# Causal attention and a product-key expert layer on one core: score products over 64 rows with one copy of the keys, and one mask product for each bank

## The reference

```
q, k, v = split((x @ w_qkv.T), 16 heads of 8)
q = rope(rms_norm(q, q_norm_w)); k = rope(rms_norm(k, k_norm_w))
attn = einsum('bhqd,bhkd->bhqk', q, k) * 8 ** -0.5
attn = where(causal, -inf, attn); attn = softmax(attn)
out = einsum('bhqk,bhkd->bhqd', attn, v) @ w_proj.T
x = layernorm(x + out)
# expert layer: xn = rmsnorm(x); q = xn @ w_q.T; s1, i1, s2, i2 = top 8 of 32 keys on two sides;
# fs = top 8 of the 64 sums; hidden = gelu(xn . expert_down[fi]) * relu(fs); y = sum hidden * expert_up[fi]
x = layernorm(x + y)
```

## Time and profile before

| | |
|---|---|
| median of 3 runs | 1785.13 us |
| the profiled execution, and its span | 1787.43 us, 1785.5 us |
| DVE busy | 1507.0 us, 84% |
| PE busy | 1353.2 us, 76% |
| ACT busy | 938.5 us, 53% |
| POOL busy | 750.4 us, 42% |
| mean granted PE clock | 0.818 of 2.4 GHz |

### The profile page before, as it was taken

The page is one execution under the profiler, slowest core; times in us unless marked ns, Lnnn a source line. Parts: engine busy times, 40 slices in busy tenths (PEclk is TensorE's granted clock), DMA queues, the critical chain, the costliest instruction groups (busy, mean ns, idle before and its releaser), DMA issues. The chain is left out here.

```text
span 1785.5 us, 53337 instructions
## 1 busy us (share of the span) xinstructions
PE 1353.2 (76%) x19632; PEld 929.3 (52%) x19632; DVE 1507.0 (84%) x6821; ACT 938.5 (53%) x1646; POOL 750.4 (42%) x1088
## 2 busy tenths in 40 slices
PE   3557588787968778796877869697887869688556
PEld 2323265554646555464645646474655546465436
DVE  2136898989899898989989899998989998988994
ACT  0647463755556475564647465564737555563110
POOL 1216353444635353453525355463534446352320
PEclk7688879797888879788887969888796978878665
DMA  3000000000000000000000000000000000000000
GB/s 77 1 6 8 6 8 8 14 8 1 15 7 15 7 14 8 1 15 7 15 7 14 8 2 15 6 15 7 15 8 14 8 1 15 1 15 1 8 7 9
DMA packets 29976, 18.59 MB, mean 10 GB/s; under 512 B 1824, under 2 KB 29216, under 8 KB 29728
## 3 DMA queue, kind: packets, MB, share of 16 engines
q1 hardware_dynamic: 29728, 15.23, 3.0%
HBM read 11.04 MB, written 4.19 MB: 9 GB/s over the span
## 5 line engine op out<-in xcount | busy, mean ns | idle before, releaser
L585 ACT ACTIVATE prob<-S 128x512 f32<-128x512 f32 x640 | 367.0, 598 | 298.8 <-PE OV L790 160.4
L869 PE MATMUL G<-whot,onehot 128*128 128x16 bf16 x12288 | 378.4, 172 | 48.3 <-DVE hid L1266 27.6
L869 PEld LDWEIGHTS G<-whot,onehot 128*128 128x128 bf16 x12288 | 365.7, 100 | 81.5 <-issue 23.5
L1228 DVE TENSOR_TENSOR onehot<-lo_no,esel 128x1024 bf16<-128x1024 uint16 x512 | 373.9, 785 | 0.2 <-issue 0.2
L422 POOL TENSOR_TENSOR qk_a<-qk_n,cosw 128x256 f32<-128x256 f32 x64 | 59.4, 928 | 482.6 <-DVE qk_n L1047 446.6
L839 PE MATMUL F<-xn,downT 128*128 128x512 f32 x256 | 153.9, 758 | 96.1 <-ACT hid L530 96.1
L777 PE MATMUL S<-causal,ident_b 128*128 128x128 bf16 x1024 | 209.1, 236 | 2.3 <-issue 2.3
L468 POOL TENSOR_TENSOR gat<-gat,cande 128x1280 f16<-128x1280 f16 x64 | 151.4, 2366 | 110.4 <-DVE gat L1189 110.4
L775 PE MATMUL S<-qT,kT_even 128*128 128x512 bf16 (+3 forms) x512 | 154.1, 332 | 50.9 <-ACT prob L585 42.3
L727 PE MATMUL S<-ident_b,stack 128*128 128x128 bf16 x1024 | 94.6, 261 | 106.1 <-POOL stack L438 72.9
L1169 DVE FIND_INDEX8 topi<-topv,sims 128x8 uint16<-128x32 f32 x1024 | 166.2, 185 | 0.0
(11 more groups left out here) (136 smaller groups left out, 2608.6 us busy)
## 6 DMA issues: line engine op xcount, KB each, us to landing
xa<-in_L_attn_x SPq DMA_DIRECT2D x16, 256.0 KB, 2.8
xr<-in_L_attn_x SPq DMA_DIRECT2D x16, 256.0 KB, 2.9
out<-r SPq DMA_DIRECT2D x16, 256.0 KB, 2.9
onehot<-in_L_ffn_expert_down SPq DMA_DIRECT2D x1, 512.0 KB, 5.9
up<-in_L_ffn_expert_up SPq DMA_DIRECT2D x1, 512.0 KB, 7.0
onehot<-in_L_ffn_keys SPq DMA_DIRECT2D x1, 256.0 KB, 6.3
onehot<-in_L_attn_w_qkv SPq DMA_DIRECT2D x1, 192.0 KB, 4.7
onehot<-in_L_attn_w_proj SPq DMA_DIRECT2D x1, 64.0 KB, 4.6
```

The costliest lines, as they stand in the source:

```text
L585: act.activation(dst, src, ACT.Exp, scale=SCALE).then_inc(exp_done.sem, 1)
L869: last = nc.tensor.matmul(bank[:, 16 * i:16 * i + 16], onehot[:, pair, t, :], whot[:, t, w_part, :], start=(w_part == 0), stop=(w_part == 2))
L1228: dve.tensor_tensor(onehot[:, pair, t:t + 8, :].rearrange("p t (c i) -> p t c i", i=2), lo, e, ALU.is_equal)
```

## The change

The keys are kept once, in `kT`, in the same layout as `qT`. A score product now reads only the 64 rows of its head, of `kT` and of `qT` (rows 0 to 63 for an even head, 64 to 127 for an odd one). ACT copies the keys of a quarter with one instruction of 128 partitions in place of two with 64. DVE no longer fills the two zero halves at the start.

`SCORES` now has all 10 units of a group. The two heads that share units are both even or both odd: heads 0 and 2 in the first five units, heads 1 and 3 in the last five, so all products of a unit read the same rows. The exponentials write to the places in `prob` that go with it. Where a bank has two blocks, both score products come first (only the first with `start`), and then a single mask product of 2 x 128 columns adds `causal` at both diagonals; it reads all 128 rows, as before. The path for far scores (`shift_by_maxima`) gets the row slices too.

```diff
-        kT = [sb("kT_even", [P, NPAIR, T], bf16), sb("kT_odd", [P, NPAIR, T], bf16)]
+        kT = sb("kT", [P, NPAIR, T], bf16)
...
-        SCORES = [[(0, 0, 0)], [(0, 1, 0), (0, 3, 384)], [(0, 2, 0), (1, 2, 256)],
-                  [(1, 0, 0)], [(1, 1, 0), (1, 3, 384)]]
+        SCORES = [[[(odd, 0, 0)], [(odd, 1, 0), (odd, 3, 384)], [(odd, 2, 0), (odd + 2, 2, 256)],
+                   [(odd + 2, 0, 0)], [(odd + 2, 1, 0), (odd + 2, 3, 384)]] for odd in range(2)]
+        SCORES = SCORES[0] + SCORES[1]
...
-                act.activation(kT[0][0:64, :, t * P:(t + 1) * P], src[0:64], ACT.Copy)
-                act.activation(kT[1][64:128, :, t * P:(t + 1) * P], src[64:128], ACT.Copy).then_inc(kT_done.sem, 1)
+                act.activation(kT[:, :, t * P:(t + 1) * P], src, ACT.Copy).then_inc(kT_done.sem, 1)
...
-                    j = 2 * g + u // 5
                     bank = S[n % 2]
-                    for half, kc, col in SCORES[u % 5]:
-                        pe_k = kT[half][:, j, kc * P:(kc + 1) * P]
-                        nc.tensor.matmul(bank[:, col:col + T - kc * P], pe_k, qT[:, j, kc * P:T],
-                                         start=True, stop=False, skip_group_check=True)
-                        last = nc.tensor.matmul(bank[:, col:col + P], ident_b[:, :], causal[:, :],
-                                                start=False, stop=True, skip_group_check=True)
-                    last.then_inc(s_ready.sem, 1)
+                    blocks = SCORES[u]
+                    for head, kc, col in blocks:
+
+                        j, rows = 2 * g + head // 2, slice(64 * (head % 2), 64 * (head % 2) + 64)
+                        nc.tensor.matmul(bank[:, col:col + T - kc * P], kT[rows, j, kc * P:(kc + 1) * P],
+                                         qT[rows, j, kc * P:T], start=(col == 0), stop=False, skip_group_check=True)
+
+                    if len(blocks) == 2:
+                        diagonal = bank[:, :].rearrange("p (c n) -> p c n", n=P)[:, 0:NT:blocks[1][2] // P]
+                        mask = causal[:, :].unsqueeze(1).to_broadcast([P, 2, P])
+                    else:
+                        diagonal, mask = bank[:, 0:P], causal[:, :]
+                    nc.tensor.matmul(diagonal, ident_b[:, :], mask, start=False, stop=True, skip_group_check=True)\
+                        .then_inc(s_ready.sem, 1)
...
-            dve.memset(kT[0][64:128, :, :], 0.0)
-            dve.memset(kT[1][0:64, :, :], 0.0)
```

More of the change, by code:

```diff
@@ L576, in exps @@
                     act.wait_ge(s_ready.sem, s_ready.value(b, n + 1))
-                    h = 2 * (u // 5)
+                    blocks = SCORES[u]
+                    head, kc, _ = blocks[0]
                     src = S[n % 2][:, :]
-                    if u % 5 == 2:
-                        dst = prob[:, h:h + 2, KC_AT[2]:KC_AT[2] + 256]
+                    if kc == 2:
+                        dst = prob[:, head:NG:2, KC_AT[2]:KC_AT[2] + 256]
                         src = src.rearrange("p (h n) -> p h n", h=2)
                     else:
-                        h, at = (h + u % 5 // 3, 0 if u % 5 in (0, 3) else 512)
-                        dst = prob[:, h, at:at + 512]
+                        dst = prob[:, head, KC_AT[kc]:KC_AT[kc] + 512]
                     act.activation(dst, src, ACT.Exp, scale=SCALE).then_inc(exp_done.sem, 1)
@@ L742, in shift_by_maxima @@
                             pe.wait_ge(peak_done.sem, peak_done.value(b, n))
-                        nc.tensor.matmul(A[:, 0:keys_up_to], qT[:, h // 2, t * P:keys_up_to],
-                                         kT[h % 2][:, h // 2, 0:keys_up_to], start=True, stop=False,
+                        rows = slice(64 * (h % 2), 64 * (h % 2) + 64)
+                        nc.tensor.matmul(A[:, 0:keys_up_to], qT[rows, h // 2, t * P:keys_up_to],
+                                         kT[rows, h // 2, 0:keys_up_to], start=True, stop=False,
                                          skip_group_check=True)
```

## The result

| | before | after |
|---|---|---|
| time, median of the runs (us) | 1785.8 | 2056.6 (2039.5 to 2059.5, 4 runs) |
| profiled execution: time, span (us) | 1787.4, 1785.5 | 2056.5, 2054.6 |
| mean granted clock over the span (share of 2.4 GHz) | 0.82 | 0.70 |
| start-to-start of line 849 / 858, "period" (us) | 102.7 | 122.9 |
| first unit to line 849 / 858, "steps" (us) | 42.0 | 61.7 |

The changed kernel takes 1.150 times as long, 95% interval 1.148 to 1.153. I had forecast 1834 us and a range from 1750 to 1880. The last three rows are taken over the steady iterations, the third to the thirteenth of the 15 periods: medians for period and steps, the mean for the clock. The iteration that I had followed before, lies with its 41.6 us and 0.96 on the good side of them.

The account below looks back on a forecast made before the run. A loop over DVE and PE was taken as the bound. Row changes +5.5 us, key copies -2.0: +3.5 us in 14 iterations, +49 us, with the first two sequences at 0, forecasting 1834 us, range 1750 to 1880.

Parts of the forecast that it names:

- the case of 1.2 GHz: Clock falls in the 40 steps; score and mask products take 24 us, not 12, per sequence; about 2000 us; chance 0.05.
- The drain: In each attention unit, PE going from 128 rows to 64 and back loses 0.22 us per pair, bounds 0 to 0.34.
- a cheap way in (0.08) and a dear way back (0.17): Around `attend`, gaps lost in us when PE's columns change from 128 to 9 and back, used as nearest evidence for rows.
- 27 x 0.19 - 0.4 - 2.0: Per period: 27 unit pairs, plus 0.3 for 7 others, less 0.7 PE wait for `hid`, less 2.0 for key copies.
- Part 1: Dropping ACT's second key copies lets first parts start at POOL's rotation end; transposes and first unit 2.0 us earlier each period.
- the fill: First two sequences: nothing covers the key copies, -4 us each, -8 in all; row changes add +4 us each, net 0.
- Part 2: Merged mask products on PE: 24 fewer products per sequence save some 3 ns each, 0.1 us, neglected.
- a gain ends at DVE: Shortening PE's list gains at most 1.5 us at line 1210 and part of 0.6; after that DVE alone bounds.
- The first rival: Row changes on PE cost nothing: -1.8 us in 14 iterations, -8 us in the first two sequences, 1752 us; chance 0.28.
- The late mask product: Sign of being right: mask product starts 0.13 us or more after a 128-column last score product, in place of 0.06.
- DVE's wait at the selection of 4 us or more: Sign of being right: DVE's wait for PE at line 1210 grows to 4 us or more from 2.0 per sequence.
- The distance of 105.5 us and 47 us for the steps: Sign of being right: two line 849 about 105.5 us apart, the 40 steps some 47 us in place of 41.6.

Follow-up runs that it names:

- merged variant: Kernel before with only merged mask products and units by even and odd heads, two key copies kept, products over 128 rows: 1783.3 us, ratio 0.999.
- 128-row variant: Changed kernel with score products over all 128 rows of kT and qT, so both heads' scores are added up: 1774.3 us, ratio 0.994 to the kernel before.

## Why the prediction was wrong

**The failed step is the clock: the forecast's sum had no term for it.** I priced the 40 steps at their granted clock of 0.96 and kept the case of 1.2 GHz as a rival at 0.05, about 2000 us. Against it I wrote that "the weights products between the units stay as they are", and took that as reason for the clock to stay. It isn't one. The weights products did stay, and the clock went to 0.59 (the variants with 64, 66 and 128 rows show by what). That rival was the right mechanism and too small in one respect: it slowed only score and mask products, 12 us for each sequence. The columns of these took 6.8 us more in the 40 steps up to the selection, since a part of them still ran at 2.4 GHz. But the clock is one for all of PE: the lines of `attend`, similarities, turned outputs and weights products, which the rival left out, are 11.1 us longer (some of it ways in to score products). With the drains, the period became 20 us longer, where the rival had 15.5.

**The drain was sized about right.** 0.22 us for a pair was forecast, bounds 0 to 0.34; measured were 0.21 us at 1.2 GHz and 0.19 at 2.4. The rule of the Trainium skill, TensorEngine Tiling (Array Packing), Key Properties, that a change of the tiling mode drains TensorE, agrees with the traces for rows too, with 0.10 us each way. The reckoning by pairs holds as well: with gaps and full rows, the period grew by 6.2 us for 34 pairs of 0.20 where the clock did not fall. What I had from the columns, a cheap way in (0.08) and a dear way back (0.17), does not carry over: 95 and 106 ns. Had the clock stayed, 27 x 0.19 - 0.4 - 2.0 = +2.7 us each period would have given 1823 us by my sum. The step was right and was not what decided.

**Part 1 was right in its mechanism and smaller.** The first parts start when POOL's rotation has ended, as forecast:

```profile
1086.04 0.84 ACT L554 ACTIVATE stack<-gat 128x768 bf16<-128x768 f32 x1 [0.33 <-POOL gat L429]
```

The transposes of quarter 2 start 50.56 us after the selection (1092.79 - 1042.23) in place of 51.88 (955.24 - 903.36): 1.3 us, not 2.0, because POOL's rotation itself ends 1.3 us later in the iteration than before, and now it is what ACT waits for. From there to the first unit it is 10.6 us in place of 8.5, 1.7 of the difference in the branch, and so the first unit comes 0.8 us later than before. With full rows the transposes did come the forecast 2.0 us earlier (median 49.8 us after the selection, 51.9 before). In the fill the gain is seen only with full rows (5.7 us until the first selection; 8 forecast); in the changed kernel the units of the first sequences run on a slower clock as well (0.68 from 65 to 130 us, where it was 0.79), and the selection is 14.9 us late where I had +4 - 4 = 0.

**Part 2, the merged masks at nothing, was right** (ratio 0.999 of the merged variant).

**That a gain ends at DVE was wrong in a way I could not see from one iteration.** The first rival had -1.8 us for each period where rows cost nothing. The 128-row variant is that case: same period, 0.6% faster, in part from the fill, and no faster at all with its code moved. DVE's wait for the selection did not shrink to POOL's gather; in 10 iterations it is

```profile
DVE hot_hi L1217 <- PE F L860: 17.7, 10, 2.4
```

where it had been 20.1.

**The signs that I had named.** The late mask product: seen (the distance from a 128-column score product to its mask is 0.15 us at 2.4 GHz, median, where 0.13 or more was asked for and 0.055 was there before). DVE's wait at the selection of 4 us or more: seen, 6.1. But it was not the largest: the wait for the turned attention outputs is 10.4 us, since these come from the slowed steps. The distance of 105.5 us and 47 us for the steps: 122.9 and 61.7. A reader of these two numbers alone would have put it on drains of 0.7 us each; the mean granted clock of the same window tells otherwise.

What stays open is how rows and gaps add up to what the chip grants. The runs show that each lowers the clock in the steps, 66 rows from 0.90 to 0.74 and gaps to 0.83 on the mean. Both together give 0.59, or 0.68 with the code moved, where the two losses added would give 0.67. A quarter of the rows fewer, or half of the units, do little (0.88 and 0.86, one run each). They show no rule that would give 0.59 from the list of products.

## What to carry to other kernels

On PE, the price of an instruction depends on whether the clock stays up around it. So a product over half of the rows is not free even though its columns, and its duration alone, are the same, and keeping zeros in the other half can be the cheaper way (by 12 to 15% here). Where a stretch is bound by PE at a high granted clock, price a change of it a second time at 1.2 GHz for everything in the stretch, and try one variant with full rows and wrong sums before rebuilding the layout. And where a loop holds its period while terms of 2 us come and go, a sum by terms does not give the gain; only a run does.

## What the hardware showed that I had not expected

- Products over 66 rows, without any gap, lowered the granted clock in the steps from 0.90 to 0.74; products over 96 rows hardly did (0.88). Zeros in half of 128 rows left it at 0.93.
- 64 rows and 128 rows in turn cost 0.10 us at each change; 66 and 128 rows in turn cost no more than 5 ns for a unit.
- The same branch at the end of PE's loop took 2.1 us or 0.36, by where the code lies: 96 short instructions ahead of it changed it. In one kernel that was worth 61 us, in another it lost 16, in a third nothing.
- Periods take few values. The changed kernel had 116.1 to 116.3 or 122.7 to 122.9, and 119.7 once; with the branch 1.7 us shorter most of them went from the higher to the lower.
